# Layer 1's inverse root of q's and k's sums of squares: GpSimd's power in place of ScalarE's square root and VectorE's reciprocal

## The reference

```python
def _l2norm(x):
    n = jnp.sqrt(jnp.sum(x * x, axis=-1, keepdims=True))
    return x / jnp.maximum(n, EPS_NORM)          # EPS_NORM = 1e-12
...
x1 = _ln(x) * (scale1 + 1.0) + shift1
qkv = (x1 @ mat_qkv_w.T + qkv_bias).reshape(B, L, 3, H, hd)
q, k, v = [jnp.transpose(qkv[:, :, i], (0, 2, 1, 3)) for i in range(3)]
sm = jnp.exp(jnp.minimum(scale_mul, MAX_SCALE_MUL))
q = _l2norm(q) * sm
k = _l2norm(k)
scores = jnp.einsum('bhqd,bhkd->bhqk', q, k)
probs = jax.nn.softmax(scores, axis=-1)
```

## Time and profile before

| what | us |
|---|---|
| median of 3 runs | 1164.55 |
| lowest and highest of the 3 runs | 1160.1, 1164.67 |
| span of the profiled execution, first to last instruction | 1160.9 |
| PE busy in it | 1094.3 |
| ACT busy in it | 800.4 |
| DVE busy in it | 706.6 |
| POOL busy in it | 491.9 |

### The profile page before, as it was taken

One profiled execution on the slowest core, in us unless ns is written; L12 is line 12 of the kernel. 1 busy time (PEld: TensorE's weight loads), 2 busy tenths in 40 slices (PEclk: granted clock), 3 DMA queues, 4 the chain that ended last, 5 costly groups with the idle time before them and its releaser, 6 DMA issues.

```text
span 1160.9 us, 19685 instructions
## 1 busy us (share of the span) xinstructions
PE 1094.3 (94%) x6717; PEld 703.3 (61%) x6717; DVE 706.6 (61%) x1484; ACT 800.4 (69%) x1336; POOL 491.9 (42%) x447
## 2 busy tenths in 40 slices
PE   8899999889898999999999999999999999999985
PEld 5576877655555565656657656566656566555442
DVE  6554447535256266234775865865865866898874
ACT  3563655477788778787687686687687686686763
POOL 3542742613543623644335553335344345254222
PEclk9999999899999999999999999999999999999997
DMA  7000001213222203321122231023031121232301
GB/s 234 20 26 28 2 10 31 62 38 94 60 64 73 75 1 82 84 58 35 28 75 73 69 83 42 15 65 82 23 88 29 39 55 51 56 84 55 83 12 36
DMA packets 36385, 64.45 MB, mean 56 GB/s; under 512 B 7208, under 2 KB 22312, under 8 KB 36288
## 3 DMA queue, kind: packets, MB, share of 16 engines
q1 hardware_dynamic: 36288, 63.20, 20.6%
HBM read 22.90 MB, written 2.12 MB: 22 GB/s over the span
## 4 chain that ended last, share of the span: by engine, by line
PE 73%; DVE 10%; ACT 8%; issue 6%; POOL 4%; POOLq 0%; ACTq 0%; DVEq 0%
PE rings L597 13%; PE AVB L709 13%; PE rings L598 11%; PE rings L599 11%; PE rings L696 10%; PE rings L671 5%; DVE m L1203 2%; PE rings L729 2%; ACT probs L891 2%; PE rings L734 2%; PE rings L640 1%; ACT L891 1%; DVE m L1183 1%; ACT gT_h L957 1%; PE rings L746 1%
## 5 line engine op out<-in xcount | busy, mean ns | idle before, releaser
L1203 DVE TENSOR_REDUCE m<-rings 128x1 fp32r<-128x512 f32 x512 | 319.0, 681 | 100.6 <-PE rings L671 73.3
L891 ACT ACTIVATE probs<-rings 128x512 f32<-128x512 f32 x562 | 292.9, 616 | 99.4 <-PE rings L671 71.1
L696 PE MATMUL rings<-SQ,SK 64*128 64x512 f32 x768 | 237.9, 446 | 14.7 <-ACT probs L888 6.3
L671 PE MATMUL rings<-SK,SQ 63*128 63x512 f32 x512 | 200.3, 457 | 5.4 <-ACT probs L891 4.2
L696 PEld LDWEIGHTS rings<-SQ,SK 64*128 64x128 f32 x768 | 109.0, 188 | 142.4 <-issue 55.1
L709 PE MATMUL AVB<-probs,V 128*32 128x512 f32 x1536 | 193.6, 611 | 0.0
L1306 POOL TENSOR_TENSOR gT_l<-gT_f,gT_h 128x512 fp32r<-128x512 f32 x96 | 121.4, 1286 | 75.7 <-ACT gT_h L957 73.8
L888 ACT ACTIVATE probs<-rings 128x1024 f32<-128x1024 f32 x103 | 101.0, 1037 | 34.2 <-PE rings L696 20.6
L597 PE MATMUL rings<-w_h,gT_h 128*128 128x256 f32 x384 | 110.2, 287 | 1.2 <-ACT gT_h L957 0.7
L671 PEld LDWEIGHTS rings<-SK,SQ 63*128 63x128 f32 x512 | 84.2, 184 | 39.7 <-ACT probs L891 33.1
L598 PE MATMUL rings<-w_l,gT_h 128*128 128x256 f32 x384 | 106.7, 278 | 0.0
(11 more groups left out here) (185 smaller groups left out, 2229.4 us busy)
## 6 DMA issues: line engine op xcount, KB each, us to landing
SQ<-qh SPq DMA_DIRECT2D x96, 128.0 KB, 2.6
SK<-kh SPq DMA_DIRECT2D x96, 128.0 KB, 2.8
SQ<-ql SPq DMA_DIRECT2D x48, 128.0 KB, 2.7
SK<-kl SPq DMA_DIRECT2D x48, 128.0 KB, 2.9
raw<-in_w SPq DMA_DIRECT2D x20, 256.0 KB, 2.8
wmod_s<-in_wmod SPq DMA_DIRECT2D x6, 512.0 KB, 4.1
gates<-gate_rows SPq DMA_DIRECT2D x12, 256.0 KB, 3.6
raw<-in_wqkv SPq DMA_DIRECT2D x9, 256.0 KB, 2.8
```

Source lines behind the costliest of these rows:

```text
L671: mm = pe.matmul(o[:, :], SQ[a % 4][r:r + KS, n // 2, c * P:(c + 1) * P], SK[a % 4][r:r + KS, n // 2, :], start=True, stop=True)
L696: mm = pe.matmul(o[:, :], SK[a % 4][r:r + KS + 1, n // 2, c * P:(c + 1) * P], SQ[a % 4][r:r + KS + 1, n // 2, :], start=True, stop=True)
L891: act.activation(probs[:, n % PROBS, :], bank(kind, a, i)[:, :], ACT.Exp, scale=SCALE[layer(unit_job(a))]).then_inc(done["scores"], 1)
L1203: nc.vector.tensor_reduce(m16[:, col:col + 1], bank(kind, a, i)[:, :], AX_X, ALU.max, negate=True).then_inc(done["max"], 1)
```

## The change

The step `qkroot` keeps DVE's clamp. Its root moves from ACT to GpSimd, as one `tensor_tensor` with the operation `pow` over 128 x 128 elements, whose exponent is the minus a half of `mhalf`, broadcast over 32 columns. It gives the inverse root at once, so DVE's reciprocal is left out. GpSimd waits for the clamp (`ss_ready`), and from the second job on also for the `kbar` of the job before, which reads `rs`.

```diff
                     act.activation(sq[:, :], qk[:, i, :], ACT.Square).then_inc(sq_ready, 1)
-                elif kind == "qkroot":
-
-                    act.wait_ge(ss_ready, nth(kind, a))
-                    act.activation(rs[:, :, :], ss[:, :, :], ACT.Sqrt).then_inc(done[kind], 1)
                 elif kind in ("q", "k"):
...
                     dve.wait_ge(done["qkroot"], nth("qkroot", a))
-                    link(nc.vector.reciprocal(rs[:, :, :], rs[:, :, :]))
                     dve.wait_ge(done["headscale"], 1)
...
+                elif kind == "qkroot":
+
+                    pool.wait_ge(ss_ready, nth(kind, a))
+                    if nth(kind, a) > 1:
+                        pool.wait_ge(kbar_ready, CH * (nth(kind, a) - 1))
+                    nc.gpsimd.tensor_tensor(rs[:, :, :], ss[:, :, :], mhalf[:, 0:TT].unsqueeze(2).to_broadcast([P, TT, 2 * HEADS]),
+                                            ALU.pow).then_inc(done[kind], 1)
```

## The result

The changed kernel takes 1242.76 us (median of 4 runs, 1241.67 to 1243.55) against 1164.61 us for the kernel before (median of 4). The ratio is 1.0672, with a 95% interval of 1.0643 to 1.0701: 6.7% slower, 78.2 us. The forecast was 1269 us, in a range of 1190 to 1281 us. The profiled spans are 1160.9 us before and 1241.1 us after, 80.2 us apart. In each run of the changed kernel the time is 1.8 us above the span, and the median before is 3.65 us above the profiled span: so the execution profiled before was about 2 us quicker than the median, and differences between the two traces hold these 2 us.

What follows compares the result with a forecast made beforehand. The prediction took PE to bound the kernel, waiting on the clamp-to-tiles stretch. Four powers of 27.6 us, less 7.0 and 2.7, plus 4 for the clock gave +104.7 us: 1269 us, range 1190 to 1281 us.

Steps and rivals of the forecast that it cites:

- The price of one power: GpSimd's power over 128 columns in jobs 4 to 7: bounds 1.31 and 27.6 us, 27.6 us taken.
- the upper end: GpSimd's power: all surplus over ordinary instructions is paid per column, 0.214 us each, 27.6 us a power; chance 0.62.
- half and half: Rival on GpSimd's power: surplus part set-up, part per column; half gives 14.3 us, 1216 us in all; chance 0.24 (5 to 22 us).
- the case of 5 to 22 us: One GpSimd power lasts between 5 and 22 us, surplus partly set-up and partly per column; chance 0.24.
- likeliest case: Whole program with the power's surplus paid per column: 1269 us, within 1250 to 1281 us; chance 0.62.
- the quarter case: GpSimd's power with a quarter of its surplus per column: 7.7 us a power, +25 us, 1190 us in all.
- The flat rival: GpSimd's power has its surplus as set-up only: 1.31 us, 4.5 us faster without the clock's term; chance 0.12.
- 4T - 7.0: PE's delay at q's and k's transposes over jobs 4 to 7, in us, with T one power's duration.
- The clock: PE restarts at 1.2 GHz after each stall in jobs 4 to 7: 1 us each, +4 us (bounds 0 and 12.8).
- ScalarE's gift: With table loads gone, ACT copies q sooner after the transposes: 0.9 us in each of jobs 5 to 7, -2.7 us.
- Nothing to make up later: During each power in jobs 4 to 7 the whole core stands; PE has no other work, so the delay stays.
- The other rival: ACT's table loads don't go, or others come; against it, ACT's order shows 43 loads instead of 50; no chance given.

Runs made afterwards that it cites:

- the four widths: Changed kernel with GpSimd's power over 128, 64, 32 and 16 columns in jobs 4 to 7, other columns a constant 0.1: 1199.95 us.
- the filled stall: Changed kernel with 80 or 88 extra products on TensorE ahead of its wait for q's tiles in jobs 4 to 7: 1235.44 us, ratio 1.0608.

## Why the prediction was right

**The price of one power** was the step that decided. The choice of the upper end gave the right sign and most of the size: 0.159 us a column by the runs, where the prediction took 0.214. The prediction drew its set-up of 0.18 us from ordinary instructions and put all the rest on four columns; by the line through the four widths the set-up of a power is 0.35 us. This one term was too big by 27.6 - 20.7 = 6.9 us a power, 27.5 us in the sum, and the whole miss is 26.5 us (104.7 forecast, 78.2 measured).

So the power lies between the upper end and the rival called half and half. In the prediction's own split, where T = 1.04 us + f x 26.6 us for a share f of the surplus that is paid by the column, 20.7 us means f = 0.74: about three quarters by the column, the rest set-up. That rival was right that both have a part, and its shares of a half and a quarter were too low. By the prediction's own bounds 20.7 us falls into the case of 5 to 22 us, which had a chance of 0.24, and 1242.76 us lies under the 1250 us at which its likeliest case began; the range held because it reached down to the quarter case. The reason given for the upper end, that such a set-up is seen in no ordinary row, gave the right order of size and not the split; the trace of before has the power at one width only, which can't give it. That the sign came out right was thus a bet on other instructions of GpSimd, and in part luck; the prediction had priced the other end at 0.12. The flat rival is ruled out by the four widths.

Beside it stood the rule of the Trainium skill, GPSIMD Engine Reference, section 3.1, of about 2.6 cycles an element. By it the power would take 0.46 us (the prediction's estimate from that page) and the kernel would be faster. The product over 128 columns, 0.40 us, agrees with that roughly; the power, 20.73 us, does not, and the measurement decides: of the operations run here the rule fits the ordinary ones and not the power.

**The path.** With 20.7 us the prediction's formulas give delays of 19.0, 18.6, 19.0 and 19.3 us in jobs 4 to 7. From clamp to transposes the two traces differ by 18.9 (24.52 against 5.58), 18.6, 18.8 and 19.2 us. 4T - 7.0 was right to 0.3 us.

**The smaller terms.** The clock was taken at +4 us and ScalarE's gift at -2.7 us, +1.3 us together. Beside the four delays of 75.7 us the medians leave 78.2 - 75.7 = 2.5 us for both. That is a remainder, and it holds the error of the medians too (runs of the kernel before lie between 1160.1 and 1169.1 us). How it splits is not shown: the 7.3 us of the filled stall can hold more than the four stalls, as said there, so they can't be set against it. ScalarE's gift is there in kind. With the stall filled, the copy of q starts 0.69 us behind the first transposes in jobs 4 to 7, where it was 1.55 to 1.60 us in jobs 5 to 7 before, so the 0.9 us a job came. In the changed kernel the copy starts after 1.12 us, as the transposes themselves run at the lower clock; the two terms are not independent, which the prediction left out. That the sum came so near says little of either term.

**Nothing to make up later** held: TensorE's idle time ahead of the transposes was 19.56 to 21.6 us, and of the 78.2 us by which the program is longer, 75.7 are those four delays.

**The other rival**, loads that don't go, fell: ACT has 43 table loads in the trace, and its busy time fell by 9.3 us, where 10.2 were worked out. That removal, with the reciprocals, is worth 4 us without any price. A replacement for the root would therefore have to cost less than about 1 us in each of the four places (an estimate, 4 us over four) to beat the kernel before, and of the versions that keep the inverse root none does.

## What to carry to other kernels

An instruction's cost on a small tile says little until it is split into set-up and price per column; two widths of the same operation give the split, and one run with four widths shows that it is a line. GpSimd's power takes 1.04 us for 4 columns and 20.7 us for 128, and a long one costs even where nobody waits for it, since GpSimd's other work queues behind it. Work that looks costly in an engine's busy time, here 10.2 us of table loads and roots and 3.8 us of reciprocals, is worth only what the path gives back when it is gone: 4 us. And a run that mends one loss, like the filled stall, may mend others of the same kind with it; what it gains is then no clean measure of the one.

## What the runs showed of the hardware

GpSimd's power costs 0.35 us and 0.159 us for each column of 128 partitions, the same within 0.5% for exponents of -0.5 and -1, for a constant base and for a broadcast operand (20.73 to 20.82 us), and 52 times as much as a product in the same shape (0.40 us). TensorE's stall of some 20 us left the granted clock at the 1.2 GHz level; in job 5 it was still there 4 us after the restart, and keeping TensorE busy through the stall with products that nobody reads made the program 7.3 us shorter.
